# VectorE's order at the end of an attention step: the residual in front of a pair's two normalised halves

## The chip, the cores and the metric

The kernel runs on one core of one Trainium2 chip. A core has five engines that each take their own instructions in program order and wait for one another by semaphores: TensorE (PE: matmuls; PEld is its weight load), VectorE (DVE), ScalarE (ACT), GpSimd (POOL) and SyncE (SP, which issues DMA transfers). The metric is the device time of one execution in microseconds. Three runs of the kernel before gave 1203.12, 1201.24 and 1200.85 us, median 1201.24.

## The reference

Sixteen batches of 100 tokens with 256 features go through four blocks. Each block normalises x, transforms it, scales it by a tanh gate and adds it to x:

```
x = x + tanh(g_xattn[0]) * L0_xattn(layernorm(x), ctx)      # first attention
x = x + tanh(g_ffn[0])   * L0_ffn(layernorm(x))             # 8 experts, top 2
x = x + tanh(g_xattn[1]) * L1_xattn(layernorm(x), ctx)      # second attention
x = x + tanh(g_ffn[1])   * L1_ffn(layernorm(x))             # shared expert + 15 experts, top 3

def L1_xattn(x, xa):                       # 16 heads of 16
    q, k, v    = split(x @ Wqkv + bqkv)
    _, ka, va  = split(xa @ Wqkv_aux + bqkv_aux)
    h_main = softmax(q k^T / 4) v          # over the 100 own tokens
    h_aux  = softmax(q ka^T / 4) va        # over the 361 context tokens
    out = h_main * (1 - sigmoid(g)) + h_aux * sigmoid(g)
    return out @ Wo + bo
```

## The kernel before, in words

The whole program is four stages that overlap a little at their borders: first attention, first experts, second attention (`attend1`), second experts. Only the second attention is touched. It works through one batch a step, in steps t = -1 to 19, of which those around t = 0 to 16 do the work. On a batch b it does, spread over several steps: layernorm and transposition of x, projections to q, k, v, scores by query (`by_query`, L1438, for the row maxima), scores by key (`by_key`, L1458, closed by L1464 that subtracts the maxima), exponents (ScalarE, L1286), sums over values (L1480), division and mixing (VectorE, L1134 to L1154), the output projection `project_out` (TensorE, L1487 on `at_wo`), and at last the residual (VectorE, L1159), which adds tanh times the projection's result to x.

The order of every engine is written out by hand. In step t VectorE does `take_max(t)` (L1107, tile `at_shift`), the maxima of batch t+1 in four parts (`maxima`, L1100 and L1101, two pairs of reductions a part), between them the division and mixing of batch t-1 and values of batches t and t+1, then `normed(t + 4)` (L1090, the layernorm of a later batch for this attention, every fourth step with a four-instruction refinement `newton`, L1079 to L1085, ahead of it), and at the end `residual(t - 1)`. The next step opens with `take_max(t + 1)` and `maxima(t + 2, 0)`.

The second experts need the layernorm of the finished x. That work, the functions of `Prepared`, is put into the attention's steps for pairs of batches. `pair_at(t + 1)` gives pair p in every second step: t = 4, 6, 8, 10, 12, 14, 16 and 18 for p = 0 to 7. Its parts are `prep.moments` on VectorE (L1799 to L1804), `prep.root` on GpSimd (L1809, a power of -0.5), then `prep.normed` on VectorE: a Newton step for the root (four instructions L1815 to L1818, each waiting for the one before) and two subtractions with a product, one a batch (L1824, tile `ex_xhat`). Behind that come ScalarE's scaled copy (`scale_normed`, L2027), GpSimd's two additions to x (`add_normed`, L2031 and L2034), a DMA of the normalised rows to memory (`keep`), TensorE's transposes (`turn`, L1834), and the router's products (`logits`, L1848). When all eight pairs are through, VectorE selects the experts (L1895 and on) and TensorE ranks the tokens (L1920, L1924).

TensorE's small results share two PSUM banks in a fixed rotation (the ring; `into(name, b)` waits until the use two places back is taken). The order per step is max, key0, key1, xT, sum_main, sum_aux, own, value01, value2, value_own, out. So the place behind `out` and `max` is key0 (`project_key`, L1391; in steps 12 to 14 it is value01, L1487 on `at_wkv_aux`): TensorE can't start it before VectorE's residual has taken `out`. The key scores of part 0 (`by_key(t, 0)`) stand behind key0 and need the first half of `maxima(t + 1, 0)`, since they go into a score bank that it reads.

Of the kernel before, what the change touches and what calls it, by code (L numbers as in the profile page):

```python
# [46 lines left out]
def on(b):  # L47

    return not isinstance(b, int) or 0 <= b < B
# [18 lines left out]
def pair_at(t):  # L68

    p = (t - 5) // 2  # L70
    return p if t % 2 == 1 and 0 <= p < PAIRED else None
# [836 lines left out]
def attend1(nc, m, consts, psum, xs, prep, early, fed, first, second):  # L908

    ident, mhalf, tanhg = consts.ident, consts.mhalf, consts.tanhs[:, 1:2]  # L910
    GB, NG = 4, B // 4
# [144 lines left out]
    def vector(dve):  # L1056
# [117 lines left out]
        for t in STEPS:  # L1174
# [32 lines left out]
            p = pair_at(t + 1)  # L1207
# [23 lines left out]
            if t > 0 and on(t + 4):  # L1231
                if (t + 4) % GB == 0:
                    newton((t + 4) // GB + 1)
                normed(t + 4)
            p = pair_at(t + 1)
            if p is not None:
                prep.normed(dve, p)
            if on(t - 1):
                residual(t - 1)
            if t == 2:  # L1240
                second.leave(dve)

# [436 lines left out]
class Prepared:  # L1679
# [2 lines left out]
    fill: Callable  # L1682
    root: Callable
    moments: Callable
    normed: Callable
    keep: Callable
    turn: Callable
# [13 lines left out]
def experts(nc, m, consts, psum, xs, name, x_out, router, router_b, pack1, pack2, b2, top, ff, shared):  # L1701
# [106 lines left out]
        pool.wait_ge(stats_ready, p + 1)  # L1808
        pool.tensor_tensor(r0[:, at], var[:, at], mhalf[0:T, :].to_broadcast([T, 2]), ALU.pow).then_inc(root_ready, 1)  # L1809

    def normed(dve, p):
        at = of_pair(p)
        dve.wait_ge(stats_ready, p + 1)
        dve.wait_ge(root_ready, p + 1)
        norm_then(dve, dve.tensor_tensor(newt[:, at], r0[:, at], r0[:, at], ALU.mult))  # L1815
        norm_then(dve, dve.tensor_tensor(newt[:, at], newt[:, at], var[:, at], ALU.mult))
        norm_then(dve, dve.tensor_scalar(newt[:, at], newt[:, at], -0.5, 1.5, ALU.mult, ALU.add))
        norm_then(dve, dve.tensor_tensor(rstd[:, at], r0[:, at], newt[:, at], ALU.mult))  # L1818
        need(dve, xhat_saved[p % XR], 16 * (p // XR))
        need(dve, turned, 2 * (p - XR + 1))  # L1820
        if shared:
            need(dve, sx_ready, p - XR + 1)
        for b in (2 * p, 2 * p + 1):
            dve.tensor_scalar(xhat[:, b % (2 * XR), :], xs[:, b, :], mv[:, b, 0:1], rstd[:, b:b + 1],  # L1824
                              ALU.subtract, ALU.mult).then_inc(xhat_ready, 1)

    def keep(sp, p):
        sp.wait_ge(xhat_ready, 2 * p + 2)
# [200 lines left out]
    def add_normed(pool, p):  # L2029
# [4 lines left out]
        pool.tensor_tensor(xs[:, of_pair(p), :], xs[:, of_pair(p), :], sb2[0:T, :].unsqueeze(1).to_broadcast([T, 2, D]), ALU.add).then_inc(base_step, 1)  # L2034

    opening = None if shared else routing(m, 1)
    prep = Prepared(load, fill, root, moments, normed, keep, turn, take_turn, logits, take_logits, scale_bias, scale_normed, add_normed,
                    turn_taken, logits_taken, opening)

    def main(m, early=None):  # L2040
# [512 lines left out]
```

## Time and profile before

| | us |
|---|---|
| median of three runs (lowest, highest) | 1201.24 (1200.85, 1203.12) |
| the profiled execution | 1201.2 |
| its span | 1199.4 |
| PE busy | 1144.2 (95%) |
| DVE busy | 624.3 (52%) |
| ACT busy | 475.3 (40%) |
| POOL busy | 391.8 (33%) |

The span runs from the first to the last instruction of the profiled execution; 1.8 us of its time lie outside. The second attention covers about 560 to 905 us of the span, and the first residual of it (t = 1) starts at 598.41 us, the last (t = 16) at 896.25 us. A busy TensorE counts pipelined matmuls, and the ends of matmuls are modelled, so starts are the safer reading. Between matmul groups PEld and PE often show short gaps put down to "issue", in which the engine waited for nothing that the profile shows.

### The profile page before, as it was taken

The page shows a single profiled execution, that of the slowest core. Times are in us where ns is not written, and L with a number is a line of the kernel's source. Part 1 is how long each engine was busy: PE and PEld are TensorE (multiplying, and loading weights), DVE is VectorE, ACT ScalarE, POOL GpSimd, SP SyncE. Part 2 cuts the span into 40 slices and gives each one's busy share as a digit, 9 for nine tenths or more (in the row PEclk, how much of TensorE's full clock was granted, in tenths as well). Part 3 has the DMA queues.
Part 4 walks back from the last instruction along what each step waited for, and adds up shares of the span by engine and source line. Part 5 has one row for each costly group of instructions (what it writes and reads, how often), then busy time and mean ns, then how long its engine had stood idle before and what let it go on. Part 6 is the DMA issues. An engine that isn't in the chain of part 4 may idle for free. (4 is left out here: it accounts for less than half of the span.)

```text
span 1199.4 us, 28945 instructions
## 1 busy us (share of the span) xinstructions
PE 1144.2 (95%) x11273; PEld 884.0 (74%) x11273; DVE 624.3 (52%) x1501; ACT 475.3 (40%) x1114; POOL 391.8 (33%) x413
## 2 busy tenths in 40 slices
PE   6999999977999999998999999999988999999998
PEld 4677777755999999985566666666655589999975
DVE  5777777776211111127887777678777412222226
ACT  3555555532333333314554454545454233333321
POOL 3676766642222222122000110110121255555410
PEclk9999999986999999999999999999999999999999
DMA  6001111403999899834012100100001379999965
GB/s 184 27 26 33 33 34 33 136 16 127 383 329 331 327 327 330 318 102 113 2 31 74 33 21 15 34 9 4 7 16 60 128 259 353 351 358 350 342 205 175
DMA packets 64391, 180.92 MB, mean 151 GB/s; under 512 B 10176, under 2 KB 36608, under 8 KB 55808
## 3 DMA queue, kind: packets, MB, share of 16 engines
q1 hardware_dynamic: 55088, 156.40, 38.3%
q0 software_dynamic: 8064, 22.03, 5.1%
q8 instruction: 91, 1.49, 0.5%
q10 hardware_dynamic: 1104, 0.64, 0.2%
q14 instruction: 44, 0.36, 0.1%
HBM read 163.11 MB, written 15.93 MB: 149 GB/s over the span
## 5 line engine op out<-in xcount | busy, mean ns | idle before, releaser
L2334 ACT ACTIVATE ex_hT<-kept_psum,ex_w 128x128 f32<-128x128 f32 x464 | 132.7, 369 | 294.8 <-PE kept_psum L2389 294.8
L2389 PE MATMUL kept_psum<-ex_xT,ex_w 128*128 128x128 f32 x1856 | 222.6, 276 | 0.0
L2296 DVE TENSOR_TENSOR ex_yt<-kept_psum,ex_b 128x256 f32<-128x256 f32 x84 | 35.7, 425 | 353.7 <-PE kept_psum L2400 353.7
L2389 PEld LDWEIGHTS kept_psum<-ex_xT,ex_w 128*128 128x128 f32 x1856 | 215.6, 193 | 0.3 <-DMA ex_w<-in_pack_in 0.2
L2400 PE MATMUL kept_psum<-ex_w,ex_hT 128*128 128x256 f32 x928 | 213.9, 379 | 0.0
L2400 PEld LDWEIGHTS kept_psum<-ex_w,ex_hT 128*128 128x128 f32 x928 | 170.1, 190 | 19.7
L2262 POOL DMA_INDIRECT ex_results<-ex_yt,ex_to_row x84 | 83.0, 988 | 254.6 <-DVE ex_yt L2296 254.6
L1286 ACT ACTIVATE at_probs<-kept_psum 120x800 f32<-120x800 f32 (+2 forms) x128 | 101.2, 841 | 97.0 <-PE kept_psum L1464 97.0
L1101 DVE TENSOR_REDUCE at_negmax<-kept_psum 100x2 f32<-100x722 f32 x128 | 115.4, 902 | 0.0
L570 ACT ACTIVATE at_probs<-kept_psum 120x800 f32<-120x800 f32 (+1 forms) x96 | 80.1, 836 | 73.3 <-PE kept_psum L693 73.2
L412 DVE TENSOR_REDUCE at_negmax<-kept_psum 120x8 bf16<-120x800 f32 (+1 forms) x96 | 90.6, 985 | 23.0 <-PE kept_psum L684 22.4
L331 POOL TENSOR_TENSOR at_sum<-at_probs 120x800 f32<-120x800 f32 (+1 forms) x47 | 76.8, 1634 | 74.7 <-ACT at_probs L570 74.5
L2255 POOL DMA_INDIRECT ex_xt<-ex_normed,ex_from_row x84 | 81.8, 974 | 50.5 <-DVE ex_from_row L1989 25.4
L1100 DVE TENSOR_REDUCE at_negmax<-kept_psum 100x2 f32<-100x200 f32 x128 | 46.4, 362 | 53.4 <-PE kept_psum L1438 52.1
L1809 POOL TENSOR_TENSOR ex_r<-ex_var,kept_mhalf 100x2 f32<-100x2 f32 x16 | 11.3, 705 | 185.6 <-DVE ex_var L1804 185.6
L1438 PE MATMUL kept_psum<-at_kT,at_qz 32*100 32x461 f32 x512 | 66.1, 585 | 3.3 <-ACT at_probs L1286 2.1
L1458 PE MATMUL kept_psum<-at_qz,at_kT 32*120 32x200 f32 (+2 forms) x1024 | 60.7, 350 | 5.2 <-DVE at_negmax L1101 4.6
L693 PE MATMUL kept_psum<-at_negmax,at_identb 120*120 120x400 bf16 (+1 forms) x192 | 50.4, 345 | 7.5 <-DVE at_negmax L412 7.5
L1458 PEld LDWEIGHTS kept_psum<-at_qz,at_kT 32*120 32x120 f32 (+2 forms) x1024 | 40.9, 173 | 20.3 <-issue 16.2
L641 PE MATMUL kept_psum<-at_ctx,at_wk 128*128 128x361 f32 x128 | 47.9, 499 | 7.6 <-DMA at_bk<-in_L_xattn_bk 6.8
L1487 PE MATMUL kept_psum<-at_wkv_aux,at_ctx 128*120 128x256 f32 (+1 forms) x192 | 48.9, 393 | 0.9 <-DVE ex_yt L2296 0.9
L659 PE MATMUL kept_psum<-at_wv,at_ctx 128*120 128x256 f32 (+1 forms) x192 | 48.3, 387 | 0.0
(256 smaller groups left out, 1674.5 us busy)
## 6 DMA issues: line engine op xcount, KB each, us to landing
ex_w<-in_pack_in SPq DMA_DIRECT2D x32, 1028.0 KB, 6.6
ex_w<-in_pack_out SPq DMA_DIRECT2D x32, 1024.0 KB, 7.7
ex_w<-in_pack_in SPq DMA_DIRECT2D x52, 514.0 KB, 5.4
ex_w<-in_pack_out SPq DMA_DIRECT2D x52, 512.0 KB, 6.1
at_ctx<-in_ctxT SPq DMA_DIRECT2D x31, 361.0 KB, 3.6
ex_normed<-ex_xhat SPq DMA_DIRECT2D x16, 200.0 KB
ex_w<-ex_results SPq DMA_DIRECT2D x6, 400.0 KB
ex_sw<-in_L_ffn_sW SPq DMA_DIRECT2D x2, 1024.0 KB
```

Of the source, the lines that this page charges most:

```text
L331: pool.tensor_tensor(sum2[0:r, :, :], p[:, :, 0:T2], p[:, :, T2:T], ALU.add).then_inc(sum2_done, 1)
L412: dve.tensor_reduce(negmax[0:r, half, :].rearrange("p (s h) -> p s h", h=HS), by_head, AX, ALU.max, negate=True).then_inc(max_done, 1)
L570: act.activation(probs[t % 2][0:r, j, half * HH:(half + 1) * HH, :].rearrange("p (s h) t -> p s (h t)", s=2), score_pair(t, j, half)[0:r, ...
L1101: dve.tensor_reduce(by_strip[:, :, HS + u], pair[0:T, :, T:KEYS], AX, ALU.max, negate=True).then_inc(max_done, 1)
L1286: act.activation(probs[b % 2][0:r, u, half * HH:(half + 1) * HH, :].rearrange("p (s h) t -> p s (h t)", s=2), score_pair("k", b, u, half)[ ...
L1438: last = pe.matmul(score_pair("q", b, u, strip // 2)[0:T, strip % 2, 0:KEYS], qz[b % NQ][rows, i, a, :], kT[b % NK][rows, i, :], start=Tru ...
L1458: pe.matmul(score_pair("k", b, u, strip // 2)[0:r, strip % 2, i * 2 * T:(i + 1) * 2 * T], kT[b % NK][rows, i, k0:k0 + r], qz[b % NQ][rows, ...
L2255: pool.indirect_dma_start(xt[t % GATHERS][:, :], None, xhd, bass.IndirectOffsetOnAxis(from_row[:, t:t + 1], 0)).then_inc(gathered[t % GATH ...
L2262: pool.indirect_dma_start(ways, bass.IndirectOffsetOnAxis(to_row[:, t:t + 1], 0), yt[t % SCATTERS][:, :], None).then_inc(scattered[t % SCA ...
L2334: last = act.activation(hT[t % N][:, c, :], ps_h[:, (t * U + u) % N, i * P:(i + 1) * P], ACT.Gelu, bias=w1[t % N][:, B1 + c:B1 + c + 1])
L2389: last = pe.matmul(ps_h[:, (t * U + u) % N, i * P:(i + 1) * P], w1[t % N][:, c * ff + f:c * ff + f + P], xT[t % N][:, c, :], start=(c == 0 ...
L2400: last = pe.matmul(ps_y[:, t % N, 0:D], hT[t % N][:, c, :], w2[t % N][:, c * D:(c + 1) * D], start=(c == 0), stop=(c == FC - 1))
```

## The change

`prep.normed` is split into `prep.newton` (the four small instructions) and `prep.whiten` (the two large ones), and VectorE's residual of batch t-1 moves in front of them. In the steps where the attention's own `newton` also runs (t = 4 and 8, `refines`) the residual goes in front of both parts; in the other pair steps (t = 6, 10, 12, 14, 16) it goes between `prep.newton` and `prep.whiten`. Step 18 has no residual. The waits of `normed` go with their parts: for moments and root with `newton`, for free `xhat` slots with `whiten`. The first attention calls the two parts one behind the other, as before. No instruction is added or removed, and TensorE, ScalarE, GpSimd and SyncE have the orders they had.

```diff
             p = pair_at(t + 1)
+            refines = t > 0 and on(t + 4) and (t + 4) % GB == 0
...
+            if refines and on(t - 1):
+                residual(t - 1)
             if p is not None:
-                prep.normed(dve, p)
-            if on(t - 1):
+                prep.newton(dve, p)
+            if not refines and on(t - 1):
                 residual(t - 1)
+            if p is not None:
+                prep.whiten(dve, p)
...
-    def normed(dve, p):
+    def newton(dve, p):
...
+    def whiten(dve, p):
         need(dve, xhat_saved[p % XR], 16 * (p // XR))
...
+    def normed(dve, p):
+        newton(dve, p)
+        whiten(dve, p)
```

VectorE at the end of step t = 4, before (a row is a line of the kernel, the operation, output and inputs; `ex_` tiles belong to the second experts, `at_` tiles to the attention):

```order
743 L1090 TENSOR_SCALAR at_xhat_241<-kept_x,at_mv,at_rstd 100x256
744 L1815 TENSOR_TENSOR ex_newt<-ex_r_203 100x2
745 L1816 TENSOR_TENSOR ex_newt<-ex_newt,ex_var 100x2
746 L1817 TENSOR_SCALAR ex_newt<-ex_newt 100x2
747 L1818 TENSOR_TENSOR ex_rstd<-ex_r_203,ex_newt 100x2
748 L1824 TENSOR_SCALAR ex_xhat<-kept_x,ex_mv,ex_rstd 100x256 x2
749 L1159 SCALAR_TENSOR_TENSOR kept_x<-kept_psum,kept_tanhs,kept_x 100x256
750 L1107 TENSOR_TENSOR at_shift<-kept_psum,at_lane 128x400
```

The same place in the changed kernel, where the lines of `prep` are 7 to 9 higher:

```order
743 L1090 TENSOR_SCALAR at_xhat_241<-kept_x,at_mv,at_rstd 100x256
744 L1159 SCALAR_TENSOR_TENSOR kept_x<-kept_psum,kept_tanhs,kept_x 100x256
745 L1822 TENSOR_TENSOR ex_newt<-ex_r_203 100x2
746 L1823 TENSOR_TENSOR ex_newt<-ex_newt,ex_var 100x2
747 L1824 TENSOR_SCALAR ex_newt<-ex_newt 100x2
748 L1825 TENSOR_TENSOR ex_rstd<-ex_r_203,ex_newt 100x2
749 L1833 TENSOR_SCALAR ex_xhat<-kept_x,ex_mv,ex_rstd 100x256 x2
750 L1107 TENSOR_TENSOR at_shift<-kept_psum,at_lane 128x400
```

The residual has moved up past six instructions; `at_shift` has kept its place. At the end of step t = 16, the last with a residual, VectorE has before:

```order
1125 L1154 STREAM_TRANSPOSE at_mixT<-at_mix 128x256
1126 L1815 TENSOR_TENSOR ex_newt<-ex_r_203 100x2
1127 L1816 TENSOR_TENSOR ex_newt<-ex_newt,ex_var 100x2
1128 L1817 TENSOR_SCALAR ex_newt<-ex_newt 100x2
1129 L1818 TENSOR_TENSOR ex_rstd<-ex_r_203,ex_newt 100x2
1130 L1824 TENSOR_SCALAR ex_xhat<-kept_x,ex_mv,ex_rstd 100x256 x2
1131 L1159 SCALAR_TENSOR_TENSOR kept_x<-kept_psum,kept_tanhs,kept_x 100x256
1132 L1799 BN_STATS ex_stats<-kept_x 100x6 x2
```

and in the changed kernel:

```order
1125 L1154 STREAM_TRANSPOSE at_mixT<-at_mix 128x256
1126 L1822 TENSOR_TENSOR ex_newt<-ex_r_203 100x2
1127 L1823 TENSOR_TENSOR ex_newt<-ex_newt,ex_var 100x2
1128 L1824 TENSOR_SCALAR ex_newt<-ex_newt 100x2
1129 L1825 TENSOR_TENSOR ex_rstd<-ex_r_203,ex_newt 100x2
1130 L1159 SCALAR_TENSOR_TENSOR kept_x<-kept_psum,kept_tanhs,kept_x 100x256
1131 L1833 TENSOR_SCALAR ex_xhat<-kept_x,ex_mv,ex_rstd 100x256 x2
1132 L1806 BN_STATS ex_stats<-kept_x 100x6 x2
```

Here the residual has moved past the two `ex_xhat` instructions only, as in steps 6, 10, 12 and 14.

## Rows read from the trace of the kernel before

**Rows 1.** The waits from 590 to 906 us: total, times, longest us.

```profile
PEld kept_psum L1391 <- DVE kept_x L1159: 9.5, 10, 1.7
```

**Rows 2.** Timeline, end of step 5 (no pair): start, length, what [idle before <-releaser].

```profile
683.66 1.11 PE L1487 MATMUL kept_psum<-at_wo,at_mixT 128*100 128x256 f32 x4
684.81 0.48 DVE L1159 SCALAR_TENSOR_TENSOR kept_x<-kept_psum,kept_tanhs,kept_x 100x256 f32<-100x256 f32 x1 [0.72 <-PE kept_psum L1487]
```

**Rows 3.** Timeline, end of step 6 (pair 1) and start of step 7.

```profile
705.61 1.11 PE L1487 MATMUL kept_psum<-at_wo,at_mixT 128*100 128x256 f32 x4
...
706.74 0.74 DVE L1824 TENSOR_SCALAR ex_xhat<-kept_x,ex_mv,ex_rstd 100x256 f32<-100x256 f32 x2
...
707.39 0.48 DVE L1159 SCALAR_TENSOR_TENSOR kept_x<-kept_psum,kept_tanhs,kept_x 100x256 f32<-100x256 f32 x1
...
707.78 0.56 DVE L1107 TENSOR_TENSOR at_shift<-kept_psum,at_lane 128x400 bf16<-128x400 f32 x1
...
707.92 1.48 PE L1391 MATMUL kept_psum<-at_ctx,at_wkv_aux 128*128 128x361 f32 x4 [0.15 <-DVE kept_x L1159]
...
708.54 0.90 DVE L1101 TENSOR_REDUCE at_negmax<-kept_psum 100x2 f32<-100x722 f32 x1
...
709.59 0.94 PE L1458 MATMUL kept_psum<-at_qz,at_kT 32*100 32x200 f32 x16 [0.18 <-DVE at_negmax L1101]
```

**Rows 4.** Timeline, end of step 4 (pair 0, with the attention's own refinement).

```profile
660.75 1.11 PE L1487 MATMUL kept_psum<-at_wo,at_mixT 128*100 128x256 f32 x4
...
661.88 0.15 DVE L1815 TENSOR_TENSOR ex_newt<-ex_r 100x2 f32<-100x2 f32 x1
...
663.85 1.48 PE L1391 MATMUL kept_psum<-at_ctx,at_wkv_aux 128*128 128x361 f32 x4 [0.94 <-DVE kept_x L1159]
```

**Rows 5.** Timeline, end of step 12 (pair 4) and start of step 13.

```profile
836.66 1.11 PE L1487 MATMUL kept_psum<-at_wo,at_mixT 128*100 128x256 f32 x4
...
837.58 0.74 DVE L1824 TENSOR_SCALAR ex_xhat<-kept_x,ex_mv,ex_rstd 100x256 f32<-100x256 f32 x2
...
839.38 0.90 DVE L1101 TENSOR_REDUCE at_negmax<-kept_psum 100x2 f32<-100x722 f32 x1
...
840.68 0.60 PEld L1458 LDWEIGHTS kept_psum<-at_qz,at_kT 32*100 32x100 f32 x16 [0.34 <-issue]
```

**Rows 6.** Timeline, start of step 15, behind pair 5.

```profile
878.71 0.38 PE L1464 MATMUL kept_psum<-at_shift,at_sel 32*100 32x400 bf16 x4 [0.52 <-DVE at_shift L1107]
```

**Rows 7.** Timeline, from step 16 (pair 6) to pair 7.

```profile
895.07 1.08 PE L1487 MATMUL kept_psum<-at_wo,at_mixT 128*100 128x256 f32 x4
...
895.60 0.74 DVE L1824 TENSOR_SCALAR ex_xhat<-kept_x,ex_mv,ex_rstd 100x256 f32<-100x256 f32 x2
...
896.37 0.72 ACT L2027 ACTIVATE ex_scaled_normed<-ex_xhat,kept_tanhs 100x512 f32<-100x512 f32 x1 [2.44 <-DVE ex_xhat L1824]
...
897.22 0.56 PE L1834 MATMUL kept_psum<-kept_ident,ex_xhat 100*128 100x100 f32 x4 [1.08 <-ACT ex_key L1855]
...
899.74 0.71 POOL L1809 TENSOR_TENSOR ex_r<-ex_var,kept_mhalf 100x2 f32<-100x2 f32 x1
...
900.55 0.16 DVE L1815 TENSOR_TENSOR ex_newt<-ex_r 100x2 f32<-100x2 f32 x1 [2.09 <-POOL ex_r L1809]
...
902.23 0.53 PE L1834 MATMUL kept_psum<-kept_ident,ex_xhat 100*128 100x100 f32 x4 [1.00 <-DVE ex_xhat L1824]
```

**Rows 8.** Timeline, VectorE's selection of experts and TensorE's ranking behind it.

```profile
905.09 0.41 DVE L1895 TENSOR_TENSOR ex_key<-ex_key,ex_router_b 100x240 f32<-100x240 f32 x1 [3.00 <-issue]
...
917.07 0.28 PE L1920 MATMUL kept_psum<-ex_zero,ex_share 100*100 100x255 f16 x1 [0.80 <-DVEq L1913]
```

**Rows 9.** Windows: length, busy PE, PEld, DVE, ACT, POOL, granted clock, DMA share, GB/s.

```profile
905.00:917.00 12.00, 9.91 (x28) 5.15 (x28) 10.51 (x25) 7.02 (x11) 1.54 (x2) 1.00 0.01 1
265.00:270.00 5.00, 2.13 (x34) 1.57 (x27) 3.12 (x12) 0.34 (x1) 0.00 (x0) 0.92 0.17 44
270.00:275.00 5.00, 3.86 (x27) 3.33 (x25) 4.62 (x21) 1.04 (x4) 0.70 (x1) 0.50 0.02 6
```

More of the change, by code:

```diff
@@ L1684 @@
     moments: Callable
+    newton: Callable
+    whiten: Callable
     normed: Callable
@@ L2036, in experts @@
     opening = None if shared else routing(m, 1)
-    prep = Prepared(load, fill, root, moments, normed, keep, turn, take_turn, logits, take_logits, scale_bias, scale_normed, add_normed,
+    prep = Prepared(load, fill, root, moments, newton, whiten, normed, keep, turn, take_turn, logits, take_logits, scale_bias, scale_normed, add_normed,
                     turn_taken, logits_taken, opening)
```

## The prediction

> **What bounds the kernel now.** I read the page first: TensorE is busy 95% of the span, VectorE 52%. That average says little here, because the edit only moves VectorE instructions in seven steps of the second attention. So I went on to the waits of that stage. TensorE's weight load waits ten times for the residual, 9.5 us in all [rows 1]. That looks like the price of the residual's late place, and is what the edit addresses. The timeline of single steps tells whether anything hangs on it. In step 6 TensorE's key projection L1391 starts at 707.92, held by the residual. But the next group, the key scores L1458, is released at 709.59 by a maximum on VectorE, whose first half ends at 708.54 + 0.90 = 709.44 [rows 3]. VectorE reaches that maximum through an unbroken row of instructions: `ex_xhat`, residual, `at_shift`, maxima. Two conditions meet within about 0.2 us at L1458, and the one that comes last is VectorE's queue. A residual that is done earlier frees the projection. It does not shorten VectorE's row, which holds the same instructions in either order. The third view is the stage's end: in step 16 the pair's `ex_xhat` is waited for at once, by ScalarE after 2.44 us of idleness [rows 7], and there the order matters.
>
> **When the residual can start.** It needs the output projection L1487. Without a pair it starts 684.81 - 683.66 = 1.15 us behind the start of L1487, after waiting 0.72 us [rows 2]. I use starts, since the ends of matmuls are modelled. The new place costs VectorE whatever this rule leaves over, and I compare it with the start of the instruction that now stands there.
> Step 4 (step 8 repeats it): 660.75 + 1.15 = 661.90, the place is at 661.88, so VectorE waits 0.02 us [rows 4].
> Step 6 (step 10 repeats it): 705.61 + 1.15 = 706.76 against 706.74, 0.02 us [rows 3].
> Step 12 (step 14 repeats it): 836.66 + 1.15 = 837.81 against 837.58, 0.23 us [rows 5].
> Step 16: 895.07 + 1.15 = 896.22 against 895.60, 0.62 us [rows 7].
> The bounds of each such wait are 0, if the result is there sooner than the rows say, and the 0.72 us of a step without a pair. I take the differences, because start to start is the same work on the same engines.
>
> **What that costs on the path.** Steps 4, 6, 8, 10: the key scores come later by 0.02 us each, 0.08 us in sum. TensorE's projection starts earlier, by up to 0.94 us in steps 4 and 8 and 0.15 us in 6 and 10 [rows 3, 4], and TensorE then stands idle in front of L1458 instead of in front of L1391. I count no gain. ScalarE takes the key earlier, too, but its exponents wait for L1464, which is behind L1458. If the cover were no cover, the gain would be 2 x 0.94 + 2 x 0.15 = 2.2 us.
> Step 12: the first half of the maximum ends at 839.38 + 0.90 = 840.28, with the wait at 840.51. In step 6 the scores followed such an end by 709.59 - 709.44 = 0.15 us, which makes 840.66; they start at 840.68 now [rows 3, 5]. The wait is just hidden, 0 us. An earlier value projection can give no more than the remaining hundredths.
> Step 14: step 15 has no projection in that place. TensorE waits 0.52 us for `at_shift` itself [rows 6], so the 0.23 us go on the path whole.
> Step 16: `ex_xhat` starts behind the residual, at 896.22 + 0.40, where 0.40 is the distance from the residual to the next instruction, 707.78 - 707.39 [rows 3]. That is 896.62 instead of 895.60, 1.02 us later. Who waits for it: ScalarE's scaled copy at 896.37, which starts right behind it; GpSimd's two additions behind that; GpSimd's root of the last pair at 899.74, queued behind the additions; VectorE's Newton step at 900.55, idle for 2.09 us until that root; the last pair's `ex_xhat`; and TensorE's transposes at 902.23, idle for 1.00 us until those [rows 7]. Then come the logits, and VectorE's selection at 905.09, which TensorE awaits at 917.07 with 0.80 us idle [rows 8]. No link has slack, so 1.02 us reach the end. The bounds are 0 (some link has slack that the row hides) and 1.12 (0.72 + 0.40).
> The moments of the last pair also come later, since they stand behind `ex_xhat` now. The root would wait for GpSimd's additions in any case, and those move by the same 1.02 us, so this adds nothing. In steps 4 to 14 `ex_xhat` comes 0.4 us later too, behind the residual, and ScalarE's copy, GpSimd's additions and the DMA with it. In those steps TensorE transposes it only in the middle of the next step, so I cost this at nothing. Had that cover been missing, it would be 0.4 us in each of six steps.
>
> **Sum.** 0.08 + 0 + 0.23 + 1.02 = 1.33 us, made against the profiled execution (span 1199.4, time 1201.2, which is within 0.1 us of the median of the runs, 1201.24). Forecast: 1201.2 + 1.3 = 1202.5 us, 0.11% longer. With a wait of nothing anywhere and a path with slack at the end it would be 1201.2; with the full 0.72 us in each of steps 4 to 14 (4.3 us) and 1.12 at step 16 it would be 1206.6. The rows give each wait directly, so I stay near their value.
>
> **Rivals.** The first: TensorE's wait for the residual was what counted. Then L1458 follows the projection and the 2.2 us come back, and with the losses of 1.33 us the time is 1201.2 - 0.9 = 1200.3 us. For it speaks the 9.5 us total [rows 1]; against it the releaser of L1458 and the end of the maximum 0.15 us ahead of it [rows 3].
> The Trainium skill, "Perfetto Trace Analysis", section Optimization Strategies, advises to work on the engines that leave the matmul engine idle; by that rule the residual is the right thing to move, and the result would be this rival's 1200.3 us. The trace agrees that TensorE is idle there, but the idleness would only move.
> The second: step 16 has hidden slack, for instance because the selection's start at 905.09 shows 3.00 us of idleness with no named cause [rows 8]. Then only 0.31 us remain and the time is 1201.5 us.
> The third ends on the slower side. In step 16 TensorE already stands idle for 1.08 us in front of L1834 at 897.22 [rows 7], and that would become 2.1 us. Its granted clock is 1.00 there, the 2.4 GHz level. At the end of the first attention, a stretch with TensorE busy 2.13 of 5 us had 0.92, and 0.50, the 1.2 GHz level, came behind it [rows 9]. If the longer gap brought the clock down for half of the 12 us from 905 to 917, in which TensorE is busy 9.91 us [rows 9], its work would grow by 5.0 us, of which 12.0 - 9.9 = 2.1 us go into idle time: 2.9 us more, 1205.4 us. It decides once the clock reads under 1.00 between 897 and 917. Against it: TensorE is much busier here than in that earlier stretch.
> The Trainium skill, "Perfetto Trace Analysis", section Matmul Optimizations, says that the matmul engine adapts its power to its use and wants its matmuls in batches back to back; it speaks for this rival and gives no price. The trace agrees on the earlier stretch, with its 0.50.
> That the change doesn't do what it says can be excluded by its order.
>
> **How the numbers follow.** The forecast gets 0.64, the first rival 0.12, the second 0.10, the third 0.10, and 0.04 is for what I don't see. A measurement of this kernel tells about 0.2% from no change, that is 2.4 us: faster means under 1198.8 us, slower over 1203.6 us. The forecast, the first and the second rival all lie within. The third rival is slower (0.10), and so is a small part of the forecast, since one run of the kernel before already gave 1203.12: 0.14 in all. Faster needs the first rival without the losses and some luck: 0.05. Within: 0.81. The range goes from the first rival, 1200.3, to 1204.0, which is about twice the forecast's loss of 1.33 us and allows for waits that I sized too small; it leaves out the third rival.
>
> **What would show it.** Right: in steps 4 and 8 the residual stands directly behind L1090 with an idle time under 0.1 us, and L1391 starts about 0.9 us earlier relative to L1487, while L1458 is still released by L1101 and stays at the same distance from L1487 (3.98 us in step 6). In step 12 and 14 the residual shows a wait of about 0.2 us, in step 16 about 0.6 us. From L1487 in step 16 to TensorE's last transposes L1834 (7.16 us now) it takes about 8.2 us, and from there to L1920 the same 14.8 us as before. Wrong: a distance from L1487 to L1458 that shrinks by more than 0.1 us, a selection that starts no later relative to the residual of step 15, or a granted clock under 1.00 behind 897 us.

## The result, and the profile after

Eleven runs of the changed kernel gave a median of 1205.87 us (1203.02 to 1210.74), eleven of the kernel before, beside them, 1201.45 us (1199.91 to 1209.04). The ratio, taken over all runs, is 1.0031, with a 95% interval of 1.0016 to 1.0046: some 3.7 us slower, where 1.3 us had been forecast. (The two medians alone lie 4.4 us apart.) The profiled execution took 1203.31 us, with a span of 1201.4.

The page of the changed kernel, busy time by engine, shows the same work as before, with 1.5 us more of matmuls, 2.2 us more of weight loads, 1.2 us more of VectorE, and 0.9 and 0.8 us less of ScalarE and GpSimd.

```profile
PE 1145.7 (95%) x11273; PEld 886.2 (74%) x11273; DVE 625.5 (52%) x1501; ACT 474.4 (39%) x1114; POOL 391.0 (33%) x413
```

The waits of the changed kernel from 590 to 906 us (total, times, longest us) answer to [rows 1]. TensorE's weight load waits 2.5 us less for the residual. TensorE itself waits 2.7 us more for the maximum instead: the lowest row is 6.1 us now, and the middle one, of the kernel before, was 3.4 us in as many waits.

```profile
PEld kept_psum L1396 <- DVE kept_x L1159: 7.0, 10, 0.7
PE kept_psum L1458 <- DVE at_negmax L1101: 3.4, 11, 0.8
PE kept_psum L1463 <- DVE at_negmax L1101: 6.1, 11, 1.2
```

The timeline of the changed kernel at the end of step 6 answers to [rows 3]. The residual starts 1.20 us behind the projection's start and `ex_xhat` stands behind it. The key projection, L1396 here, comes directly behind and no longer waits. The key scores (L1463) still wait for the maximum. From L1492, the output projection here, to them it is 710.24 - 706.19 = 4.05 us, against 3.98 before.

```profile
706.19 1.11 PE L1492 MATMUL kept_psum<-at_wo,at_mixT 128*100 128x256 f32 x4
...
707.39 0.48 DVE L1159 SCALAR_TENSOR_TENSOR kept_x<-kept_psum,kept_tanhs,kept_x 100x256 f32<-100x256 f32 x1
707.79 0.73 DVE L1833 TENSOR_SCALAR ex_xhat<-kept_x,ex_mv,ex_rstd 100x256 f32<-100x256 f32 x2
...
708.27 1.48 PE L1396 MATMUL kept_psum<-at_ctx,at_wkv_aux 128*128 128x361 f32 x4
...
709.19 0.90 DVE L1101 TENSOR_REDUCE at_negmax<-kept_psum 100x2 f32<-100x722 f32 x1
...
710.24 0.94 PE L1463 MATMUL kept_psum<-at_qz,at_kT 32*100 32x200 f32 x16 [0.48 <-DVE at_negmax L1101]
```

At the end of step 4, which answers to [rows 4], the projection comes 1.02 us nearer to L1492 (2.08 us instead of 3.10), and its idle time has moved to the scores.

```profile
661.31 1.11 PE L1492 MATMUL kept_psum<-at_wo,at_mixT 128*100 128x256 f32 x4
...
662.45 0.48 DVE L1159 SCALAR_TENSOR_TENSOR kept_x<-kept_psum,kept_tanhs,kept_x 100x256 f32<-100x256 f32 x1
...
663.39 1.48 PE L1396 MATMUL kept_psum<-at_ctx,at_wkv_aux 128*128 128x361 f32 x4
...
666.09 0.72 PE L1463 MATMUL kept_psum<-at_qz,at_kT 32*100 32x200 f32 x9 [1.21 <-DVE at_negmax L1101]
```

Steps 12 and 14, which answer to [rows 5] and [rows 6]: here VectorE waits 0.32 us for the projection, and behind step 14 TensorE waits 0.81 us for `at_shift`, where it was 0.52.

```profile
838.61 0.48 DVE L1159 SCALAR_TENSOR_TENSOR kept_x<-kept_psum,kept_tanhs,kept_x 100x256 f32<-100x256 f32 x1 [0.32 <-PE kept_psum L1492]
...
878.09 0.48 DVE L1159 SCALAR_TENSOR_TENSOR kept_x<-kept_psum,kept_tanhs,kept_x 100x256 f32<-100x256 f32 x1 [0.32 <-PE kept_psum L1492]
...
879.76 0.38 PE L1469 MATMUL kept_psum<-at_shift,at_sel 32*100 32x400 bf16 x4 [0.81 <-DVE at_shift L1107]
```

From step 16 to pair 7, which answers to [rows 7]. The residual waits 0.68 us. ScalarE's copy waits 3.47 us instead of 2.44, and TensorE 2.11 instead of 1.08. The root, VectorE's Newton step and the last transposes have the same waits as before, so the whole chain has moved: from L1492 to the last L1847 it is 904.30 - 896.11 = 8.19 us, against 902.23 - 895.07 = 7.16.

```profile
896.11 1.08 PE L1492 MATMUL kept_psum<-at_wo,at_mixT 128*100 128x256 f32 x4
...
897.28 0.48 DVE L1159 SCALAR_TENSOR_TENSOR kept_x<-kept_psum,kept_tanhs,kept_x 100x256 f32<-100x256 f32 x1 [0.68 <-PE kept_psum L1492]
897.68 0.72 DVE L1833 TENSOR_SCALAR ex_xhat<-kept_x,ex_mv,ex_rstd 100x256 f32<-100x256 f32 x2
...
898.44 0.72 ACT L2040 ACTIVATE ex_scaled_normed<-ex_xhat,kept_tanhs 100x512 f32<-100x512 f32 x1 [3.47 <-DVE ex_xhat L1833]
...
899.30 0.57 PE L1847 MATMUL kept_psum<-kept_ident,ex_xhat 100*128 100x100 f32 x4 [2.11 <-ACT ex_key L1868]
...
901.82 0.71 POOL L1816 TENSOR_TENSOR ex_r<-ex_var,kept_mhalf 100x2 f32<-100x2 f32 x1
...
902.62 0.16 DVE L1822 TENSOR_TENSOR ex_newt<-ex_r 100x2 f32<-100x2 f32 x1 [2.08 <-POOL ex_r L1816]
...
904.30 0.54 PE L1847 MATMUL kept_psum<-kept_ident,ex_xhat 100*128 100x100 f32 x4 [0.99 <-DVE ex_xhat L1833]
```

The selection and the ranking answer to [rows 8]. From L1492 it is 11.05 us to the first and 23.03 us to the second, against 10.02 and 22.00 before: the whole delay of 1.03 us arrives.

```profile
907.16 0.41 DVE L1908 TENSOR_TENSOR ex_key<-ex_key,ex_router_b 100x240 f32<-100x240 f32 x1 [3.00 <-issue]
...
919.14 0.28 PE L1933 MATMUL kept_psum<-ex_zero,ex_share 100*100 100x255 f16 x1 [0.81 <-DVEq L1926]
```

The windows of the changed kernel behind the gap (columns as in [rows 9]) show a granted clock of 1.00, the 2.4 GHz level, throughout. In this one trace the third rival's condition was not met.

```profile
899.30:902.70 3.40, 3.40 (x19) 2.47 (x20) 1.28 (x3) 1.79 (x5) 3.14 (x3) 1.00 0.21 56
906.10:918.10 12.00, 10.41 (x37) 5.81 (x35) 9.71 (x24) 7.21 (x11) 2.51 (x2) 1.00 0.01 4
```

So the parts of this trace that the edit can reach explain some 1.5 us and the runs say 3.7. The experiments ask for the rest.

### The profile page after: what moved, and what is told of

It reads as the page before. It is cut to its first block and busy times, and to the rows that moved or that the text cites. A ratio compares the mean times of both kernels' runs of the same rounds, so it can differ in the third digit from the quotient of the medians.

```text
span 1201.4 us, 28941 instructions
## 1 busy us (share of the span) xinstructions
PE 1145.7 (95%) x11273; PEld 886.2 (74%) x11273; DVE 625.5 (52%) x1501; ACT 474.4 (39%) x1114; POOL 391.0 (33%) x413
## 5 line engine op out<-in xcount | busy, mean ns | idle before, releaser
L1463 PE MATMUL kept_psum<-at_qz,at_kT 32*120 32x200 f32 (+2 forms) x1024 | 60.7, 351 | 7.6 <-DVE at_negmax L1101 7.3
L1463 PEld LDWEIGHTS kept_psum<-at_qz,at_kT 32*120 32x120 f32 (+2 forms) x1024 | 40.9, 174 | 22.7 <-issue 18.6
L1492 PE MATMUL kept_psum<-at_wkv_aux,at_ctx 128*120 128x256 f32 (+1 forms) x192 | 48.9, 394 | 0.9 <-DVE ex_yt L2309 0.9
L684 PE MATMUL kept_psum<-at_qz,at_kT 32*120 32x200 f32 (+1 forms) x768 | 47.3, 362 | 1.4 <-ACT at_qz L561 0.7
```

The costliest lines, as they stand in the source:

```text
L1463: pe.matmul(score_pair("k", b, u, strip // 2)[0:r, strip % 2, i * 2 * T:(i + 1) * 2 * T], kT[b % NK][rows, i, k0:k0 + r], qz[b % NQ][rows, ...
```

## The experiments

For all traces I use distances between starts, in which the time at which the stage is reached drops out: A from the first residual (t = 1) to `at_shift` of step 15, B from the output projection of step 16 to the last pair's transposes, C from that projection to the ranking. The last column says where the granted clock fell to half in A or C.

| trace | A | B | C | half clock |
|---|---|---|---|---|
| before | 279.68 | 7.16 | 22.00 | none |
| before, three more (lookb1 to 3) | 279.65 to 279.77 | 7.15 to 7.17 | 21.99 to 22.00 | none |
| changed | 280.31 | 8.19 | 23.03 | none |
| again | 280.24 | 8.61 | 23.64 | behind the gap of step 16 |
| again2 | 280.26 | 8.20 | 23.04 | none |
| look1 | 280.27 | 8.19 | 23.02 | none |
| look2 | 280.14 | 8.66 | 23.71 | behind the gap |
| look3 | 281.42 | 10.02 | 25.19 | step 14; behind the gap |
| look4 | 281.44 | 8.71 | 23.75 | step 14; behind the gap |
| behind16 | 280.16 | 7.16 | 22.00 | none |
| only16 | 279.63 | 8.19 | 23.03 | none |
| warm16, warm16b | 280.11, 281.38 | 8.19, 8.21 | 23.03, 23.06 | none; step 14 |
| gap3 | 280.21 | 11.48 | 26.65 | behind the gap |
| rootfirst | 279.75 | 7.43 | 22.28 | none |
| rootfirst_new | 281.44 | 8.72 | 23.75 | step 14; behind the gap |
| hold | 279.64 | 6.00 | 21.17 | none |
| hold_new | 280.11 | 7.04 | 22.08 | none |

Behind the first 560 us the clock fell twice more outside A and C: in `rootfirst_new` at 571.5 us, before A, and in `warm16b` at 1197.0 us, 12 us ahead of its end, each time for 3.4 us and at a place whose order no edit touches. All traces also have stretches at half clock between 249 and 305 us, ahead of the second attention. "Behind the gap" is meant to about 0.2 us: in `again` and `look2` the fall is recorded 0.2 and 0.1 us ahead of the gap's end, in the others up to 0.8 us behind it.

**again: the changed kernel, no edit.** It was to tell how much of the 3.7 us comes back.

> The changed kernel once more. Theory A (queue): only VectorE's waits count, 0.3 us in steps 4 to 14 and 1.0 us at step 16, so the median is about 1.3 us over the kernel before (ratio 1.001), the mean granted clocks of the runs are like those of the kernel before, and what the first timing showed beyond that was scatter. Theory B (clock): the gap on TensorE behind step 16, 2.11 us instead of 1.08, lets the clock fall in a part of the runs; then the ratio is about 1.003 again, and about a third of the runs have a mean clock of 0.983 or less and are 3 to 6 us longer than the others.

Measured: median 1204.14 us (12 runs), 1.0009 (0.9996 to 1.0023) of the kernel before. The timing that gave 3.7 us gives about 1 us now. Theory B had expected about a third of the runs at a mean granted clock of 0.983 or less; one of twelve was. The trace brought what the first one did not have, in its windows from step 16's projection on:

```profile
899.00:902.30 3.30, 1.29 (x5) 0.58 (x4) 2.48 (x11) 0.75 (x3) 0.00 (x0) 0.99 0.00 0
902.30:905.70 3.40, 3.29 (x8) 2.07 (x9) 1.32 (x3) 1.21 (x4) 3.21 (x3) 0.51 0.23 60
```

The stretch with the gap, TensorE busy 1.29 of 3.30 us, is followed by 3.4 us at 0.51, the 1.2 GHz level. Its timeline shows where: the gap of 2.11 us, which ends with a small copy of ScalarE (`ex_key`) that stands behind the scaled copy of `ex_xhat`, and behind the gap four matmuls of 128x400 in 2.79 us (1.53 at the full clock).

```profile
899.21 1.08 PE L1492 MATMUL kept_psum<-at_wo,at_mixT 128*100 128x256 f32 x4
...
902.40 0.93 PE L1847 MATMUL kept_psum<-kept_ident,ex_xhat 100*128 100x100 f32 x4 [2.11 <-ACT ex_key L1868]
903.12 2.79 PE L2127 MATMUL kept_psum<-ex_sxT,ex_sw 128*128 128x400 f32 x4
```

The price is small, since the chain through VectorE and GpSimd covers most of it: C is 23.64 instead of 23.03, 0.6 us.

**behind16 and only16: the two halves of the edit.** In `behind16` the residual of step 16 is back behind the pair's layernorm, in `only16` it stands in front in step 16 alone: there the second line of the diff reads `behind = t < B`.

```diff
-            if refines and on(t - 1):
+            behind = t == B
+            if refines and not behind and on(t - 1):
                 residual(t - 1)
...
-            if not refines and on(t - 1):
+            if not refines and not behind and on(t - 1):
                 residual(t - 1)
             if p is not None:
                 prep.whiten(dve, p)
+            if behind and on(t - 1):
+                residual(t - 1)
```

> The changed kernel with step 16 alone put back: there the residual stands behind the two normalised halves again. Theory A: 0.3 us over the kernel before (ratio 1.0003), the distance from the projection of step 16 to TensorE's last transposes is 7.16 us again instead of 8.19. Theory B: the same, and no more runs of low mean clock than the kernel before has. A third theory C (steps 4 to 14 cost more than their rows say): ratio 1.002 or more, with the loss inside 660 to 880 us.

> The kernel before with the new order in step 16 alone. Theory A: 1.0 us over the kernel before (ratio 1.0009). Theory B: about 1.0025, with a part of the runs at a mean clock of 0.983 or less. Theory C: ratio under 1.001.

Measured: `behind16` 1203.49 us, 1.0008 (0.9997 to 1.0018); `only16` 1203.87 us, 0.9999 (0.9987 to 1.0011). The traces divide the loss cleanly. With the old order in step 16, B and C are those of before to 0.01 us, and A keeps its 0.48 us. With only step 16 changed, A is that of before to 0.05 us and B has its 1.03 us. The timings don't resolve this: `only16` comes out even although its trace has 1.03 us more, which lies within its interval (up to 1.0011, 1.3 us). I take the sizes from the traces and don't call either ratio a proof. `only16` has the gap of 2.11 us as well, and theory B had expected about 1.0025 and a part of the runs at a mean clock of 0.983 or less: the ratio lies below that, no run of twelve was at such a clock, and its trace shows no fall.

**warm16 and warm16b: the gap filled.** TensorE does 14 extra products of 128 columns (28 instructions in the trace), whose results nobody reads, behind the projection of step 16.

```diff
             if t == B + 1:
+                keep_warm(psum[:, 2, :], 14)
                 pe.wait_ge(prep.logits_taken, PAIRED - 2)
```

> The changed kernel with 14 small matmuls on TensorE, whose results nobody reads, in its gap behind the projection of step 16. The gap of 2.11 us shrinks to about 0.5 us. Theory A: no change against the changed kernel, ratio 1.001 to the kernel before. Theory B: the runs of low mean clock are gone, so the ratio falls from 1.003 to 1.001.

> The changed kernel with TensorE's gap of step 16 filled, timed once more. Its first timing gave a mean of 1204.0 us with 2 of 12 runs at a mean clock of 0.984 or less. Theory B: again at most 2 of 12, and a mean about 1.5 us over the kernel before, 0.8 us less than the changed kernel. If the low-clock runs have nothing to do with the gap: 3 or 4 of 12, and 2.4 us over the kernel before.

Measured: 1203.79 us, 1.0006 (0.9994 to 1.0018), and 1204.77 us, 1.0018 (1.0006 to 1.0030). The timeline of the first shows TensorE busy through the gap:

```profile
896.36 1.08 PE L1492 MATMUL kept_psum<-at_wo,at_mixT 128*100 128x256 f32 x4
897.27 3.29 PE L1383 MATMUL kept_psum<-at_wkv_aux,kept_ident 128*128 128x128 f32 x28
```

The products overrun the gap: the pair's transposes start 4.04 us behind the projection instead of 3.19. B doesn't grow by that, since TensorE's wait at its end shrinks from 0.99 to about 0.2 us. In neither trace does the clock fall behind step 16, and B and C stay at 8.19 to 8.21 and 23.03 to 23.06: the queue's part is there without the gap. That the filling keeps the clock up is a hint only, since with a fall behind every second unfilled gap of 2.11 us (counted below) two traces without one come by luck one time in four. The timings don't show it either: 25 runs have a mean of 1204.6, 39 of the changed kernel 1205.6, and the difference of 1.0 us is uncertain by 1.1. `warm16b` by itself speaks on both sides. Its mean is 2.5 us over the kernel before, where theory B had expected 1.5, and 2.4 if the gap has no part. Of its 13 runs one has a mean clock of 0.984 or less, as theory B had expected (at most two of twelve).

**again2, gap3: the gap made longer.** `again2` is the changed kernel beside it. `gap3` puts three additions of 128x400, which nobody reads, between residual and `ex_xhat` of step 16.

```diff
             if not refines and on(t - 1):
                 residual(t - 1)
+            if t == B:
+                for unread in (qz[1], qz[2]):
+                    dve.tensor_tensor(unread.rearrange("p c a t -> p (c a t)"), osb[0].rearrange("p g t -> p (g t)")[:, 0:4 * T],
+                                      osb[1].rearrange("p g t -> p (g t)")[:, 0:4 * T], ALU.add)
+                dve.tensor_tensor(shift.rearrange("p h t -> p (h t)"), osb[0].rearrange("p g t -> p (g t)")[:, 0:4 * T],
+                                  osb[1].rearrange("p g t -> p (g t)")[:, 0:4 * T], ALU.add)
```

> The changed kernel a third time, because its first timing gave a ratio of 1.0031 and the second 1.0009. Theory A (queue, corrected by the traces: 0.48 us in steps 4 to 14, 1.03 us behind step 16): ratio 1.0013, and whatever a run has beyond that arises before 598 us. Theory D (the change costs about 3.7 us, of which the traces that I have show only a part): ratio 1.003.

> The changed kernel with three more VectorE additions between the residual and the normalised halves of step 16, whose results nobody reads; TensorE's gap there grows from 2.11 to about 3.5 us. Theory A: 1.3 to 1.5 us over the changed kernel, all of it between the projection of step 16 and TensorE's last transposes, ratio about 1.0025. Theory B (clock): in addition the clock falls behind the gap in most runs, which costs 0.6 us or more each time; the profile shows a granted clock of 0.5 for some us behind it.

Measured: `again2` 1205.67 us, 1.0022 (1.0008 to 1.0036), which excludes neither of its two theories; `gap3` 1209.41 us, 1.0054 (1.0037 to 1.0071). The windows of `gap3` around its gap of 3.57 us:

```profile
897.50:901.10 3.60, 0.04 (x1) 0.00 (x0) 3.43 (x10) 0.84 (x3) 0.04 (x1) 1.00 0.01 4
901.10:905.00 3.90, 3.88 (x16) 2.68 (x16) 1.71 (x6) 1.60 (x4) 3.16 (x3) 0.59 0.19 49
905.00:909.00 4.00, 4.00 (x11) 2.44 (x12) 0.90 (x3) 1.00 (x4) 0.00 (x0) 0.54 0.19 51
```

The low clock lasts 6.8 us here. It reaches the logits, which the selection needs: C is 26.65. The additions lengthened the gap by 3.57 - 2.11 = 1.46 us, and C grew by 3.62, so the clock costs 2.2 us. The timings agree: six runs of `gap3` have a mean 3.6 us over that of `again2`, uncertain by 1.6, where the longer gap alone makes 1.5. This is what the third rival described, at a longer gap than the change makes.

**look1 to look4 and lookb1 to lookb3: how often.** Single traces, of the changed kernel and of the kernel before, without edits.

> The changed kernel, one more trace. Theory A: steps 4 to 14 cost 0.48 us and the stage's end 1.03 us more than in the kernel before, as in every trace of it so far. Theory B: in two of five traces with a gap of 2.11 us the granted clock fell to 0.5 for some us behind the gap or near it; if it does here, the end costs about 0.6 us more.

> The kernel before, one more trace. Theory B: with its gap of 1.08 us the granted clock stays at 1.00 from 590 to 1190 us, as in all three traces so far with this gap.

> The changed kernel, one more trace. Theory B: in about a third of such traces the granted clock is 0.5 for 3.4 us or more just behind TensorE's gap of step 16, and the distance from the projection of step 16 to TensorE's ranking is then 23.6 us instead of 23.03. Theory A: always 23.03.

> The changed kernel, one more trace, with the same question: 23.03 us (theory A, and two of three traces by theory B), or 23.6 us with a fallen clock behind the gap (theory B).

> The changed kernel, one more trace, with the same question: 23.03 us (theory A, and two of three traces by theory B), or 23.6 us with a fallen clock behind the gap (theory B).

> The kernel before, one more trace. Theory B: the clock stays at 1.00 behind step 16, 22.0 us from the projection of step 16 to the ranking. If the clock also falls here behind a gap of 1.08 us: 22.6 us.

> The kernel before, one more trace, with the same question: 22.0 us with a full clock behind step 16 (theory B), or 22.6 us. Near step 14 a fall of the clock would lengthen the part from the first residual to step 15 from 279.7 to 280.9 us; theory B says nothing of it.

Measured: changed 1203.42, 1206.21, 1208.18 and 1205.61 us; before 1200.43, 1203.08 and 1200.65. Behind the gap the clock fell in `look2`, `look3` and `look4`, not in `look1`, and in none of the kernel before. In `look3` it lasts as long as in `gap3`, with the longest price of the seven, 25.19 - 23.03 = 2.2 us. Its windows:

```profile
873.00:877.00 4.00, 2.98 (x16) 1.28 (x12) 3.52 (x10) 1.57 (x2) 0.00 (x0) 0.70 0.00 0
877.00:881.00 4.00, 3.80 (x43) 2.33 (x41) 2.83 (x11) 1.56 (x2) 0.00 (x0) 0.88 0.00 0
...
902.40:909.00 6.60, 6.60 (x20) 4.17 (x19) 1.39 (x6) 1.58 (x5) 1.92 (x2) 0.52 0.12 32
```

and its timeline, where the pair's transposes come 2.11 us late again, and the second row of products of 128x400 takes twice its time as well:

```profile
901.14 0.56 PE L1847 MATMUL kept_psum<-kept_ident,ex_xhat 100*128 100x100 f32 x4 [2.11 <-ACT ex_key L1868]
901.54 2.59 PE L2127 MATMUL kept_psum<-ex_sxT,ex_sw 128*128 128x400 f32 x4
...
905.16 3.01 PE L2127 MATMUL kept_psum<-ex_sxT,ex_sw 128*128 128x400 f32 x4
```

The first two windows show a second fall, around step 14, that makes A 1.15 us longer (281.42 against 280.27).

Counted over all traces by the gap of step 16: at 2.11 us the clock fell behind it in five of ten (four of the seven of the changed kernel, and `rootfirst_new` below); at 3.57 us in the only one; at 1.1 us or less, or filled, in none of nine. If the gap made no difference, six falls in twenty traces would all lie in those eleven about one time in 84. The seven traces of the changed kernel against the four of the kernel before alone, four falls to none, would come by chance one time in nine. The fall around step 14 came in four of thirteen traces with the new order there and in none of seven with the old. That can be chance: of such twenty traces, four falls would all lie in the thirteen about one time in seven. And just ahead of the fall, which starts at 874.6 us in `look3`, TensorE's named waits are those of the kernel before, the longest 0.8 and 1.0 us; its wait for `at_shift`, 0.3 us longer with the new order, comes only behind. In `rootfirst_new` the fall at 571.5 us came behind a wait of 1.08 us in code that no edit touches. So the clock can fall behind waits of about 1 us too, and whether the new order has a part in the fall around step 14 stays open.

**rootfirst and rootfirst_new: a shorter chain behind step 16.** The chain that the change delays runs over GpSimd's two additions, behind which the root of the last pair queues. Here the root goes first, in the kernel before and in the changed one.

```diff
             if p is not None:
                 prep.root(pool, p)
+            if b == B + 1:
+                prep.add_normed(pool, PAIRED - 2)
             p = pair_at(b + 1)
-            if p is not None:
+            if p is not None and p != PAIRED - 2:
                 prep.add_normed(pool, p)
```

> The kernel before (the residual behind the halves everywhere), with GpSimd's root of the last pair moved ahead of the two additions for pair 6. If the chain halves, scaled copy, additions, root, Newton step, halves, transposes is what leads to TensorE's last transposes, these move forward by the 1.0 us for which TensorE waits there, and no further, since its own work then bounds it: ratio 0.9992 to the kernel before. If the chain is not what bounds the stage's end: ratio 1.000.

> The changed kernel with the same move on GpSimd. If TensorE's wait for pair 6 is a second bound beside the chain through the root, the loss of 1.03 us behind step 16 stays (TensorE's first transposes are still late) while 1.0 us is won behind it: ratio 1.0005 to the kernel before. If the chain through the root were the only bound, the root would no longer depend on the halves of step 16, and the whole 1.03 us would be gone as well: ratio 0.9995.

Measured: 1202.94 us, 1.0002 (0.9985 to 1.0019), and 1206.93 us, 1.0022 (1.0008 to 1.0036). No gain, where 1.0 us had been expected: B is 7.43 where it was 7.16. The trace of `rootfirst_new` can't answer its question, since the clock fell in it; `hold_new` below does. The timeline of `rootfirst` shows why. The root ends early, but two of VectorE's small instructions last 1.15 and 1.12 us beside the additions, where the same kinds take 0.16 and 0.17 without one.

```profile
900.03 0.69 POOL L1811 TENSOR_TENSOR ex_r<-ex_var,kept_mhalf 100x2 f32<-100x2 f32 x1 [4.75 <-DVE ex_var L1806]
900.70 1.27 POOL L2033 TENSOR_TENSOR kept_x<-kept_x,ex_scaled_normed 100x512 f32<-100x512 f32 x1
900.83 1.15 DVE L1817 TENSOR_TENSOR ex_newt<-ex_r 100x2 f32<-100x2 f32 x1 [0.88 <-POOL ex_r L1811]
902.04 1.27 POOL L2036 TENSOR_TENSOR kept_x<-kept_x,ex_sb 100x512 f32<-100x512 f32 x1
902.21 1.12 DVE L1819 TENSOR_SCALAR ex_newt<-ex_newt 100x2 f32<-100x2 f32 x1
...
904.45 0.53 PE L1836 MATMUL kept_psum<-kept_ident,ex_xhat 100*128 100x100 f32 x4 [1.27 <-DVE ex_xhat L1826]
```

**hold and hold_new: the additions kept back until VectorE is through.** The root goes first again; the additions of pair 6 go one step later and wait for the last `ex_xhat`.

```diff
+            if b == B + 2:
+                prep.add_normed(pool, PAIRED - 2)
             p = pair_at(b + 1)
-            if p is not None:
+            if p is not None and p != PAIRED - 2:
                 prep.add_normed(pool, p)
...
     def add_normed(pool, p):
+        if p == PAIRED - 2:
+            pool.wait_ge(xhat_ready, B)
```

> The kernel before with GpSimd's root of the last pair first, and with GpSimd's two additions for pair 6 held back until VectorE has normalised the last pair. If rootfirst won nothing only because its additions blocked VectorE's Newton step (1.15 and 1.12 us for instructions of 0.16 us), the distance from the projection of step 16 to TensorE's last transposes falls from 7.16 to about 6.2 us, where TensorE's own work bounds it, ratio 0.9992. If another link bounds that chain: 7.2 us, ratio 1.000.

> The changed kernel with the same two moves. The distance from the projection of step 16 to TensorE's last transposes falls from 8.19 to about 7.2 us: the wait for pair 6, 1.03 us longer than in the kernel before, stays. If that wait did not count, about 6.2 us.

Measured: on the kernel before 1201.46 us (1199.92 to 1204.32, 12 runs), 0.9987 (0.9975 to 1.0000); on the changed kernel a single run, 1203.66 us. In the timeline of `hold` the small instructions take 0.16 and 0.17 us again, and the last transposes come 6.00 us behind the projection instead of 7.16.

```profile
897.03 1.08 PE L1489 MATMUL kept_psum<-at_wo,at_mixT 128*100 128x256 f32 x4
...
900.84 0.16 DVE L1817 TENSOR_TENSOR ex_newt<-ex_r 100x2 f32<-100x2 f32 x1 [0.88 <-POOL ex_r L1811]
...
901.23 0.17 DVE L1819 TENSOR_SCALAR ex_newt<-ex_newt 100x2 f32<-100x2 f32 x1
...
902.52 1.27 POOL L2035 TENSOR_TENSOR kept_x<-kept_x,ex_scaled_normed 100x512 f32<-100x512 f32 x1 [1.78 <-DVE ex_xhat L1826]
903.03 0.51 PE L1836 MATMUL kept_psum<-kept_ident,ex_xhat 100*128 100x100 f32 x4
```

`hold` has the lowest ratio of all versions here, though its interval touches 1; in the trace C is 0.83 us shorter than before. On top of the change B is 7.04: against `hold` the change's 1.04 us is still there.

This corrects the chain of the prediction in one point. In `hold_new` the last pair's root no longer waits for the additions, and yet the whole delay arrives, because TensorE carries it by itself. Its gap of 2.11 us stays, and from the transposes behind it to those of the last pair it is 904.33 - 900.49 = 3.84 us of its own work, without a wait, in `hold_new` as in `hold`:

```profile
900.49 0.56 PE L1849 MATMUL kept_psum<-kept_ident,ex_xhat 100*128 100x100 f32 x4 [2.11 <-ACT ex_key L1870]
...
904.33 0.51 PE L1849 MATMUL kept_psum<-kept_ident,ex_xhat 100*128 100x100 f32 x4
```

So two paths lead from `ex_xhat` to the end of the stage: the one over GpSimd, which the prediction follows and which is 1.0 us longer in the kernel before, and TensorE's gap. The edit delays both by the same amount.

## Why the prediction was wrong

**The time.** The forecast was 1202.5 us and the range ended at 1204.0. The measured 1205.87 lies outside, on the slower side (over 1203.6 us), which had 0.14.

**What held.** The bound of steps 4 to 14 was read rightly. TensorE's waits for the residual were no price: the projection came up to 1.02 us earlier, and L1458 of before stayed where VectorE's maxima let it be, with 3.98 us become 4.05. The first rival is refuted by that row and by the waits, 2.5 us less at the one and 2.7 us more at the next. Every term of the sum is in the traces. Steps 4 and 8: 0.02 us, as forecast. Steps 6 and 10: 0.07 instead of 0.02. Step 12: 0.28 at its end, of which the next step gives 0.25 back, hidden as argued. Step 14: 0.27 instead of 0.23. Step 16: 1.03 instead of 1.02. The rule that a residual starts 1.15 us behind the projection was up to 0.05 us short (1.20 in step 6), which is the excess there. Together that is 0.04 + 0.14 + 0.03 + 0.27 = 0.48 us, the lengthening of A in `behind16`; the first trace of the changed kernel has 0.15 us more in A, in steps 2 and 3, which the edit doesn't touch. With 0.48 + 1.03 the queue's part is 1.5 us where 1.33 was forecast. The second rival (slack behind step 16) is refuted: B and C grew by the whole 1.03 us, and `behind16` takes it back whole. The single chain that the prediction draws there is one of two, as `hold_new` shows; the delay is the same on both.

**The step that failed** is the treatment of the third rival: "Against it: TensorE is much busier here than in that earlier stretch", a chance of 0.10, and a time of its own instead of a term in the sum, which has nothing for the clock. The clock did fall behind the longer gap, in four of seven traces of the changed kernel and in none of four before. The price per fall was mis-sized too: 2.9 us was estimated, 0.6 to 0.7 us was measured in three of the four and 2.2 us in one. In `again` the waits that TensorE had behind the gap, 0.99 us in front of the last transposes among them, are gone, so a part of its slower work went into idle time. The mean over the seven traces is (0.6 + 0.7 + 2.2 + 0.7) / 7 = 0.6 us. `gap3` bears the mechanism out: with 3.57 us the clock fell and stayed low longer, and the timings show the price. `warm16` and `warm16b` fit it, but show little with two traces. "It decides once the clock reads under 1.00 between 897 and 917" was the right test, but one trace can't answer it: the first one didn't show it, and I could have taken it for excluded. The Trainium skill, "Perfetto Trace Analysis", section Matmul Optimizations, which the prediction cited for this rival, was the better guide here: the traces agree with its advice as far as the clock fell behind five of ten gaps of 2.11 us and behind none of the seven of about 1.08 us at the same place.

**What adds up and what doesn't.** 1.5 us of queue, 0.6 of clock behind step 16, and 2 of 7 traces times 1.15 = 0.3 around step 14 (cause open) make 2.5 us. Taken over all timings, 39 runs of the changed kernel have a mean of 1205.6 us and 113 of the kernel before 1202.9: 2.7 us, uncertain by 0.8, or 0.22%. That agrees. It also lies inside the interval of the first timing, which is 1.9 to 5.5 us; the three timings of the changed kernel gave 1.0031, 1.0009 and 1.0022. I take the scatter for the program's and not the edit's: the first residual, behind instructions that are alike, started between 597.8 and 604.2 us over the traces. That isn't shown in full, since it started at 599.8 us in the mean of the seven traces of the changed kernel and at 598.4 in the four of the kernel before; `only16`, `rootfirst` and `hold`, with the old order up to step 15, had it at 600.3 to 601.0.

A run's mean granted clock helps little. It was 0.983 or less in 7 of 39 runs of the changed kernel and in 4 of 102 of the kernel before (the first eleven have no clock on record), and four of the seven are the four slowest of the first timing, 1207.67 to 1210.74 us, of which none was traced. But it was so in none of the six runs of `gap3`, whose trace has 6.8 us at the low level behind step 16 and a mean clock of 0.987.

With the clock's terms the forecast would have been 1201.2 + 2.5 = 1203.7 us, still inside the range. What took this median out of it is therefore more than the failed step: the other part is the excess of this one timing, which no trace holds and whose cause stays open. So the range was also too narrow for a measured median: it allowed for waits sized too small and not for 2 us of scatter between timings (ratios of 1.0009 and 1.0031 for the same kernel), though the three runs shown already spread over 2.3 us.

## What to carry to other kernels

When one engine waits for a second in the profile, look who ends the wait behind it: here the 2.5 us saved came back at the next wait, because VectorE's row of instructions was as long as before. At the end of a stage, where a chain has no slack, an instruction that is put in front of the chain's first link costs its own distance plus its wait. Add to such a delay what it does to TensorE's clock as a term with a frequency, read from several traces, look for a second path that carries it, and give the range the scatter of whole timings.

## What the runs showed of the hardware that I had not expected

A gap of 2.11 us on TensorE, at the end of step 16, was followed by the 1.2 GHz level in five of ten traces with the same work ahead of it, one of about 1.08 us at the same place in none of seven, and one of 3.57 us in the one trace. Behind the gap of 2.11 us the low level lasted 3.4 us in four traces and 6.8 us in one. Elsewhere it also came behind waits of about 1 us: 1.08 us in `rootfirst_new` (571.5 us), and 0.8 and 1.0 us close together in four traces (step 14).

GpSimd's additions of 100x512, 1.27 us each, stretched VectorE's instructions on 100x2 from 0.16 to 1.15 us and 0.17 to 1.12 us in `rootfirst`, and the stretch is shown as duration, not as idle time. With the additions kept back, in `hold`, it is gone. The same is in both kernels themselves: `ex_var` ahead of the last root takes 0.64 us in the kernel before, shows 1.16 us in this timeline of `look3`, and 0.17 us in `hold`.

```profile
901.23 1.16 DVE L1811 TENSOR_SCALAR ex_var<-ex_mv 100x2 f32<-100x2 f32 x1
```

The Trainium skill, "SBUF — State Buffer", section SBUF: two separate sides, says that GpSimd shares a pair of ports with those VectorE instructions that have two inputs in SBUF or run in a two-port mode, and that whoever starts first holds it for its whole instruction. The trace of `rootfirst` agrees: the instruction of 1.15 us started 0.13 us behind an addition of 1.27 us and ended with it, within 0.02 us, and so did the one of 1.12 us. That the ports are the cause no run here isolates.
